# Attention keys in three bf16 parts: the stacks of parts laid out dimension by dimension, a row of ones filled by GpSimd, a batch of context requested by another queue

## The reference, cut to what matters

```python
def _L0_xattn_ref(q_vec, k_vec, v_vec, mask_input, Wq, bq, Wk, bk, Wv, bv, Wo, bo):
    ...
    q, k, v = proj(q_vec, Wq, bq), proj(k_vec, Wk, bk), proj(v_vec, Wv, bv)   # [b, head, row, 16]
    energy = jnp.einsum('bhqd,bhkd->bhqk', q, k) / jnp.sqrt(jnp.float32(D))
    energy = jnp.where(mask_input == 0, jnp.float32(-1000000000.0), energy)
    attn = jax.nn.softmax(energy, axis=-1)
    context = jnp.einsum('bhqk,bhkd->bhqd', attn, v)
    ...
x = x + _L0_xattn_ref(_layernorm(x), ctx_1024, ctx_1024, mask, ...)
x = x + _L0_attn_ref(_layernorm(x), ...)     # convolutions, gates
x = x + _L0_ffn_ref(_layernorm(x), ...)      # quantised feed forward
x = x + _L1_xattn_ref(...)                   # second cross attention
x = x + _L1_attn_ref(...)                    # attention with 16 heads of 64
x = x + _L1_ffn_ref(...)                     # 8 experts
```

## Time and profile before

| what | value |
|---|---|
| median of 3 runs | 941.09 us (939.6 to 942.02) |
| the profiled execution | 943.52 us |
| its span, first to last instruction | 941.7 us |
| TensorE busy | 893.4 us (95%) |
| VectorE, ScalarE, GpSimd busy | 605.6, 474.1, 107.8 us |
| mean granted TensorE clock | 0.986 |
| moved by DMA | 108.70 MB, mean 115 GB/s |

### The profile page before, as it was taken

One profiled execution on the slowest core, in us unless ns is written; L12 is line 12 of the kernel. 1 busy time (PEld: TensorE's weight loads), 2 busy tenths in 40 slices (PEclk: granted clock), 3 DMA queues, 4 the chain that ended last, 5 costly groups with the idle time before them and its releaser, 6 DMA issues.

```text
span 941.7 us, 15461 instructions
## 1 busy us (share of the span) xinstructions
PE 893.4 (95%) x6065; PEld 529.9 (56%) x6067; DVE 605.6 (64%) x1066; ACT 474.1 (50%) x953; POOL 107.8 (11%) x127
## 2 busy tenths in 40 slices
PE   7799799999999999999999999999999999999998
PEld 3356344444556665545445577754784884556745
DVE  5879478777886556888863387786724217459352
ACT  3242466777776566777779642314421310568311
POOL 2320011111000000000000200010100005335200
PEclk9899899999999999999999899999999999999999
DMA  9975733545322212222603620084645732000000
GB/s 294 302 223 164 219 107 96 154 122 168 107 68 80 68 34 60 76 67 70 210 8 129 259 71 1 1 266 137 223 179 187 260 100 79 1 1 1 1 0 23
DMA packets 68885, 108.70 MB, mean 115 GB/s; under 512 B 7110, under 2 KB 42950, under 8 KB 66886
## 3 DMA queue, kind: packets, MB, share of 16 engines
q1 hardware_dynamic: 65516, 100.61, 33.9%
q10 hardware_dynamic: 3296, 7.08, 2.2%
HBM read 93.77 MB, written 13.89 MB: 114 GB/s over the span
## 4 chain that ended last, share of the span: by engine, by line
PE 81%; DVE 7%; ACT 5%; DMA 3%; issue 2%; POOL 1%; SPq 0%; ACTq 0%; DVEq 0%
PE psum L1932 13%; PE psum L1914 11%; PE psum L1879 11%; PE psum L2312 6%; PE psum L1856 6%; PE psum L2340 6%; PE psum L2449 4%; PE psum L2073 4%; PE psum L1846 4%; PE psum L2086 3%; ACT arena L799 2%; PE psum L2503 2%; PE psum L2488 1%; PE psum L2527 1%; DVE arena L1202 1%
## 5 line engine op out<-in xcount | busy, mean ns | idle before, releaser
L1202 DVE TENSOR_REDUCE arena<-psum 128x1 f32<-128x1024 f32 x256 | 301.1, 1219 | 108.4 <-PE psum L1879 107.8
L799 ACT ACTIVATE arena<-psum 128x512 f32<-128x512 f32 x512 | 263.6, 603 | 68.2 <-PE psum L1914 67.0
L1879 PE MATMUL psum<-arena 96*128 96x512 bf16 x512 | 153.2, 381 | 9.5 <-DMA arena<-kparts 4.4
L1914 PE MATMUL psum<-arena 99*128 99x256 bf16 x1024 | 155.1, 274 | 3.5 <-ACT arena L790 1.2
L1932 PE MATMUL psum<-arena 128*32 128x256 f32 x2048 | 137.5, 386 | 0.1
L1914 PEld LDWEIGHTS psum<-arena 99*128 99x128 bf16 x1024 | 80.6, 97 | 98.2 <-ACT arena L799 36.7
L1932 PEld LDWEIGHTS psum<-arena 128*32 128x32 f32 x2048 | 53.5, 109 | 75.6 <-ACT arena L799 31.1
L1846 PE MATMUL psum<-arena 128*128 128x512 f32 x128 | 64.5, 632 | 11.9 <-DMA arena<-ctxT 10.5
L1879 PEld LDWEIGHTS psum<-arena 96*128 96x128 bf16 x512 | 48.9, 98 | 28.7 <-DVE arena L1202 11.4
L1856 PE MATMUL psum<-arena 128*128 128x256 f32 x256 | 64.1, 387 | 0.0
L673 POOL TENSOR_TENSOR arena<-arena 128x512 bf16<-128x512 f32 x34 | 41.4, 1217 | 196.4 <-DVE arena L1188 193.8
(11 more groups left out here) (259 smaller groups left out, 961.2 us busy)
## 6 DMA issues: line engine op xcount, KB each, us to landing
arena<-kparts SPq DMA_DIRECT2D x192, 128.0 KB, 3.1
kparts<-arena SPq DMA_DIRECT2D x32, 384.0 KB, 3.3
arena<-ctxT SPq DMA_DIRECT2D x20, 512.0 KB, 5.9
arena<-mask SPq DMA_DIRECT2D x8, 1024.0 KB, 5.4
arena<-ctx SPq DMA_DIRECT2D x2, 4096.0 KB, 17.0
arena<-mask ACTq DMA_DIRECT2D x4, 1024.0 KB, 13.9
arena<-ctxT SPq DMA_DIRECT2D x1, 4096.0 KB, 13.6
arena<-ctxT SPq DMA_DIRECT2D x4, 1024.0 KB, 9.1
```

The lines of the kernel that those rows point to most:

```text
L799: nc.scalar.activation(PR[step % 4][:, pair * CH:(pair + 1) * CH], exp_bank(step, pair), ACT.Exp)\
L1202: nc.vector.tensor_reduce(MX[g % 2][:, col:col + 1], unit_banks(n).rearrange("p b n -> p (b n)"), AX.X, ALU.max).then_inc(s_maxed, 1)
L1879: last = nc.tensor.matmul(out, q, KST[g % 2][0:ROWS, j, at], start=True, stop=not masked, skip_group_check=True)
L1914: last = nc.tensor.matmul(heads[:, u, :], KST[gg % 2][0:KROWS, j, kc * P:(kc + 1) * P], QST[0:KROWS, G * g + j, b * S:(b + 1) * S], start= ...
```

## The change

Keys and queries are projected with their features in the order dimension first, head second (`by_dim` permutes weights and biases on the host). `kparts` in HBM is now divided by quarter, with the rows of a quarter next to one another, so that the four heads of a group form one run of 4096 numbers for each dimension. The stack's rows are ordered by key part: 48 rows for the high part (dimension by dimension, three copies of each), 32 for the middle part, 16 for the low. One transfer brings all rows of a part, repeating each source row. So a quarter takes three transfers, and the queries likewise; the queries' three stores become one. The ones are no input any more: GpSimd fills them, the first time behind its other memsets, the second time behind the last low part of batch 0. The first six chunks of batch 1's context are requested by ScalarE, right behind its value copies. The matmuls keep their number and sizes.

```diff
+TWO_ONES = struct.unpack("<f", struct.pack("<I", 0x3F803F80))[0]
-K_PARTS = (0, 0, 0, 1, 1, 2)
-Q_PARTS = (0, 1, 2, 0, 1, 0)
+K_ROWS = ((0, 3), (3, 5), (5, 6))
...
-        KST = [b16(8192 * i, 16384).rearrange("p (j n) -> p j n", j=G) for i in range(2)]
+        KST = [b16(8192 * i, 16384).rearrange("p (c j n) -> p c j n", c=QUARTERS, j=G) for i in range(2)]
...
-        QST = b16(37392, 8192).rearrange("p (h n) -> p h n", h=H)
+        QST = b16(37392, 8192).rearrange("p (b h n) -> p b h n", b=B, h=H)
...
-        kparts = nc.dram_tensor("kparts", [B, 3, D, S2], BF16, kind="Internal").ap()
-        qparts = nc.dram_tensor("qparts", [3, D, T], BF16, kind="Internal").ap()
+        kparts = nc.dram_tensor("kparts", [B, QUARTERS, 3, D, 2 * CH], BF16, kind="Internal").ap()
+        qparts = nc.dram_tensor("qparts", [B, 3, D, S], BF16, kind="Internal").ap()
...
-            sp.dma_start(arena[ROWS:KROWS, 0:8192], t["ones"]).then_inc(q_stacked, 16)
...
             def store_k(b, c, f):
                 r = piece_number(b, c, f)
                 sp.wait_ge(k_low, r + 1)
-                sp.dma_start(kparts[b, :, f * P:(f + 1) * P, c * CH:(c + 1) * CH].rearrange("r p n -> p r n"),
+                sp.dma_start(kparts[b, c // 2, :, f * P:(f + 1) * P, c % 2 * CH:(c % 2 + 1) * CH].rearrange("r p n -> p r n"),
                              KPT[place(r)]).then_inc(k_stored[place(r)], 16)
...
             def load_stack(gg, quarter):
                 b, g = gg // GPB, gg % GPB
-                at = slice(quarter * 2 * CH, (quarter + 1) * 2 * CH)
-                for r in range(6):
-                    src = kparts[b, K_PARTS[r], g * G * DH:(g + 1) * G * DH, at]
-                    sp.dma_start(KST[gg % 2][r:ROWS:6, :, at],
-                                 src.rearrange("(j d) n -> d j n", d=DH)).then_inc(k_stacked[gg % 2][quarter], 16)
+                for part, (first, last) in enumerate(K_ROWS):
+                    src = kparts[b, quarter, part].rearrange("(d h) n -> d (h n)", d=DH)[:, g * G * 2 * CH:(g + 1) * G * 2 * CH]
+                    sp.dma_start(KST[gg % 2][first * DH:last * DH, quarter].rearrange("p j n -> p (j n)"),
+                                 src.unsqueeze(1).broadcast_to((DH, last - first, G * 2 * CH)))\
+                      .then_inc(k_stacked[gg % 2][quarter], 16)
...
             def store_queries(b):
                 r = query_piece(b)
                 sp.wait_ge(k_low, r + 1)
-                parts = KPT[place(r)].rearrange("p r (f n) -> p r f n", f=CT)
-                for part in range(3):
-                    sp.dma_start(qparts[part, :, b * S:(b + 1) * S].rearrange("(f p) n -> p f n", p=P), parts[:, part])\
-                      .then_inc(k_stored[place(r)], 16)
+                sp.dma_start(qparts[b].rearrange("r (f p) n -> p (r f) n", p=P),
+                             KPT[place(r)].rearrange("p r (f n) -> p (r f) n", f=CT)).then_inc(k_stored[place(r)], 16)
 
             def load_queries(b):
                 r = query_piece(b)
                 stored(r)
-                for r in range(6):
-                    src = qparts[Q_PARTS[r], :, b * S:(b + 1) * S]
-                    sp.dma_start(QST[r:ROWS:6, :, b * S:(b + 1) * S], src.rearrange("(h d) n -> d h n", d=DH))\
+                for first, last in K_ROWS:
+                    sp.dma_start(QST[first * DH:last * DH, b].rearrange("p h n -> p (h n)"),
+                                 qparts[b, 0:last - first].rearrange("r (d h) n -> d r (h n)", d=DH))\
                       .then_inc(q_stacked, 16)
...
             load_queries(1)
-            sp.dma_start(arena[ROWS:KROWS, 8192:16384], t["ones"]).then_inc(late_loaded, 16)
             sp.dma_start(BV, t["rows"][:, ROW_AT["bv"]:ROW_AT["bv"] + 256].broadcast_to((P, 256)))\
               .then_inc(late_loaded, 16)
             sp.dma_start(AW, t["A"].rearrange("(t p) s -> p t s", p=P)).then_inc(on["bm_loaded"], 16)
-            for c in range(SLOTS):
-                first_values_done(c + 2)
-                load_ctx(1, c, 0)
...
+            def ones_for_maxima(i):
+
+                nc.gpsimd.memset(arena[ROWS:KROWS, 8192 * i:8192 * (i + 1)], TWO_ONES).then_inc(built, 1)
+                pool.wait_ge(built, 9 + i)
+
+            pool.wait_ge(built, 8)
+            ones_for_maxima(0)
...
                 if idx == 2 * BRANCH - 1:
                     pool.wait_ge(q_split, 10)
                     low_part(query_piece(1), QREST)
+                if idx == 2 * NCH - 1:
+                    pool.wait_ge(k_low, r + 1)
+                    pool.wait_ge(mask_step, 8)
+                    ones_for_maxima(1)
...
             def load_queries():
 
                 act.wait_ge(k_stored[place(query_piece(0))], stores_by(query_piece(0)))
-                for row in range(6):
-                    act.dma_start(QST[row:ROWS:6, :, 0:S],
-                                  qparts[Q_PARTS[row], :, 0:S].rearrange("(h d) n -> d h n", d=DH)).then_inc(q_stacked, 16)
+                for first, last in K_ROWS:
+                    act.dma_start(QST[first * DH:last * DH, 0].rearrange("p h n -> p (h n)"),
+                                  qparts[0, 0:last - first].rearrange("r (d h) n -> d r (h n)", d=DH))\
+                       .then_inc(q_stacked, 16)
+
+            def load_next_ctx(c):
+
+                act.wait_ge(ring_drained, VALUE_AT[0, c + 2, 1] + 1)
+                n = load_number(1, c, 0)
+                act.dma_start(CTX[n % SLOTS], ctx_chunk(1, c)).then_inc(ctx_loaded[n % SLOTS], 16)
 
             for c in range(ROUNDS):
                 for i in range(2):
@@ -831,6 +844,8 @@
                         load_queries()
                     if c in VALUES_AT:
                         copy_values(0, VALUES_AT[c], i)
+                if c in VALUES_AT and VALUES_AT[c] >= 2:
+                    load_next_ctx(VALUES_AT[c] - 2)
...
-                    dve.wait_ge(late_loaded, 32)
+                    dve.wait_ge(late_loaded, 16)
...
-                    pe.wait_ge(q_stacked, 16 + 96 * (b + 1))
+                    pe.wait_ge(q_stacked, 48 * (b + 1))
                 if i % 8 == 0:
-                    pe.wait_ge(k_stacked[g % 2][quarter], 96 * (g // 2 + 1))
-                q = QST[0:ROWS, G * (g % GPB) + j, b * S + qt * P:b * S + (qt + 1) * P]
+                    pe.wait_ge(k_stacked[g % 2][quarter], 48 * (g // 2 + 1))
+                q = QST[0:ROWS, b, G * (g % GPB) + j, qt * P:(qt + 1) * P]
                 for half in range(2):
                     at = slice((2 * quarter + half) * CH, (2 * quarter + half + 1) * CH)
                     out = unit_banks(n)[:, half, :]
-                    last = nc.tensor.matmul(out, q, KST[g % 2][0:ROWS, j, at], start=True, stop=not masked,
+                    last = nc.tensor.matmul(out, q, KST[g % 2][0:ROWS, quarter, j, half * CH:(half + 1) * CH], start=True, stop=not masked,
...
                     pe.wait_ge(ring_drained, TOP_AT[gg, 1] + 1)
-                    if gg:
-                        pe.wait_ge(late_loaded, 32)
+                    pe.wait_ge(built, 10 if gg else 9)
...
-                        last = nc.tensor.matmul(heads[:, u, :], KST[gg % 2][0:KROWS, j, kc * P:(kc + 1) * P],
-                                                QST[0:KROWS, G * g + j, b * S:(b + 1) * S],
+                        last = nc.tensor.matmul(heads[:, u, :], KST[gg % 2][0:KROWS, kc // 8, j, kc % 8 * P:(kc % 8 + 1) * P],
+                                                QST[0:KROWS, b, G * g + j, :],
...
+    by_dim = np.arange(D).reshape(H, DH).T.reshape(-1)
+    cols = {"bq": a["L0_xattn_bq"][by_dim], "bk": a["L0_xattn_bk"][by_dim], "in_b": a["L0_attn_in_b"],
...
-        "wqT": c(a["L0_xattn_Wq"].T), "wkT": c(a["L0_xattn_Wk"].T), "wvT": c(a["L0_xattn_Wv"].T),
+        "wqT": c(a["L0_xattn_Wq"][by_dim].T), "wkT": c(a["L0_xattn_Wk"][by_dim].T), "wvT": c(a["L0_xattn_Wv"].T),
...
-        "ones": np.full((3, 8192), np.array([0x3F803F80], np.uint32).view(np.float32)[0], np.float32),
```

More of the change, by code:

```diff
@@ L1 @@
 import itertools
+import struct
 from contextlib import ExitStack
@@ L453, in stores_by @@
         def stores_by(r):
-            queries = sum(query_piece(b) <= r and place(query_piece(b)) == place(r) for b in range(B))
-            return 16 * (turn_at(r) + 2 * queries)
+            return 16 * turn_at(r)
         def stores_ahead(r):
@@ L705, in _ @@
             powers = [2 + 1]
-            pool.wait_ge(built, 9)
+            pool.wait_ge(built, 11)
             def power(first, last):
@@ L789, in copy_tops @@
                     act.wait_ge(ring_filled, slot + 1)
-                    nc.scalar.activation(QST[ROWS:KROWS, j:j + 2, b * S:(b + 1) * S],
+                    nc.scalar.activation(QST[ROWS:KROWS, b, j:j + 2, :],
                                          ring_heads(slot)[ROWS:KROWS], ACT.Copy).then_inc(ring_drained, 1)
@@ L2576, in _ @@
             pe.wait_ge(on["g_chosen"], 1)
-            pe.wait_ge(built, 11)
+            pe.wait_ge(built, 13)
```

(3 more changed lines are left out.)

## The result

The changed kernel takes 936.36 us (935.0 to 936.81, 6 runs), the kernel before 941.16 us (939.6 to 942.02, 6 runs). The ratio is 0.9948, 95% interval 0.9935 to 0.9961: faster by 4.8 us, where 11 were forecast. The profiled execution took 936.81 us with a span of 935.0, 6.7 us less than that of before. That execution of before lay 2.4 us above its median, so the traces differ by more than the medians; where the text follows a stretch, it follows the traces.

What follows compares the result with a forecast made beforehand. The prediction took TensorE, busy 893.4 of 941.7 us, as the bound, with gains only at its waits and low clock. Terms -5.0 - 6.6 + 0.6 = -11.0 gave a median of 930.0 us, range 926.5 to 937.

Steps and rivals of the forecast that it cites:

- B: TensorE's 4.31 us wait for context before the second batch's key projection at 109.19, plus half clock; claimed gain 6.6 us.
- The price of the last issue: ScalarE's last context issue, before the maxima copies that the product at 100.78 awaits; claimed +0.6 us, bounds 0.5 and 1.
- sign of danger: At the first turned product near 100 us: idle lengthening past 2 us and bringing the clock down would show the forecast wrong.
- GpSimd's fill: Filling 8192 words per partition twice, first from about 3.0 us; 8.4 us expected, cost 0, bounds 0 and +2.9.
- A's landing: Arrival of stacked keys and queries awaited before the first score product; claimed at 40.6 us, product then starting at 43.66.
- the term -5.0: Gain from three stack and query transfers instead of six, at the wait before the first score product; range 0 to -7.0.
- The ones: Dropping the two 96 KB transfers of ones was claimed to change nothing, as neither is in a TensorE wait.
- What is late next is VectorE: After the first score product, VectorE's splits and maxima set score unit 3; unit 4 starts at 49.9, not 54.89.
- only B goes: Rival: the first score product's wait hardly moves, because memory and engines pace it, not issues; 935 us, chance 0.17.
- The sentence from the Trainium skill on ports: Objection to the new rows: partitions 0 to 63 use 8 of 16 ports; 4.8 us for queries and quarter, landing at 41.1.

Runs made afterwards that it cites:

- e3: The kernel before with only the second batch's context moved to ScalarE's queue; 935.51 us, ratio 0.9941.
- e1: The changed kernel with the stacks' and queries' old rows and transfers, keeping GpSimd's ones and context on ScalarE's queue; 935.81 us, ratio 0.9943.
- e6: The changed kernel with six transfers of 16 rows without repetition, runs of 8 KB, written 6 partitions apart; 934.02 us, ratio 0.9923.
- e8: Old rows, GpSimd's ones and context on ScalarE's queue as in e1, plus batch 0's queries asked for earlier, at 28.7 us; 930.21 us, ratio 0.9875.
- e7: The same six transfers as e6, but each written to 16 neighbouring partitions; 937.8 us in a single run.
- e5: The changed kernel with batch 0's queries asked for earlier, behind the value copy at 28.7 us; 932.39 us, ratio 0.9904.
- e2: The kernel before with only the ones filled by GpSimd instead of transferred; 940.05 us, ratio 0.9981.
- e4: The kernel before with only the new rows, transfers and single query store; ones still transferred, context still on SP; 945.97 us, ratio 1.0063.

## Why the prediction was wrong, point by point

- **B, "Term: -6.6 us"**: right. From TensorE's end before it to the turned product behind it pass 2.81 us instead of 9.46, which is -6.65, and e3 has it alone.
- **The price of the last issue, "+0.6 us"**: right in mechanism; the idle grew by 0.42 us, with an issue of 0.38. What the term leaves out is the clock behind the longer idle. The prediction put its sign of danger at 2 us; in e1, e6 and e8 1.67 to 1.70 us were followed by the half clock and another 1.2 us.
- **GpSimd's fill, "I take 0"**: right. It took 6.92 us, not 8.4: a line through this fill and the 0.524 us of 512 words gives, as an estimate, 0.83 ns a word and a fixed 0.1 us, which the estimate had scaled too. It ended 5.9 us before the first low part.
- **The step that failed is A's landing**: "at 359 GB/s, which the window 44 to 46 shows, that is 4.4 us" and "with about 1 us to the end of the wait I put the landing at 40.6". It rested on a rate taken from a window in which no stack was loaded (44 to 46 us, packets of 1 KB on SP's queue). The new rows move at 188 GB/s where their window holds nothing else, e6 and e7 show that the partitions written decide this rate, and the queries landed at 42.9. So the term -5.0 was -0.2. Within it, "six issues take 4.1 of the 9 us" was read as a pace, which it was for the old rows only; the change took issues away and put transfers of neighbouring partitions in their place, and these took back what the longer runs gave.
- The second half of the same step: the queries were treated as landing with the stack. They are asked for at a place of their own, and once SP reached its stack 4 us earlier, its next stores came in between. e5 and e8 show that this place was worth 4 to 6 us: e5 -4.0 from the changed kernel, e8 -5.6 from e1 by the medians of different batches, -4.1 and -6.4 by the ratios.
- **The ones, "the two transfers go, at nothing: neither is in a TensorE wait"**: wrong. Not being waited for is no price. They slowed the mask's transfers and through them the stores, and SP's stack issue moved by 4.0 us (4.2 in e2, with the ones alone). In the changed kernel this gain was there and then lost at the queries, which had not moved.
- **"What is late next is VectorE"**, with unit 4 at 49.9: right where the landing was mended. In e8 it is VectorE that TensorE waits for, and unit 4 comes at 48.00. The 1.9 us between are those by which VectorE's last split before its maxima ends earlier (41.12 + 0.43 = 41.55 for 43.42), in a kernel that no longer loads the ones.
- **Rivals**: the one that came true in the main is "only B goes", 935 us at a chance of 0.17. Its reason, that memory and engines pace the landing and not the issues, comes near what the runs showed; it did not name the partitions or the place of the queries. The sentence from the Trainium skill on ports ("SBUF — State Buffer", section "Door 1: The DMA port swizzle (why `[64,N]` ≈ `[32,N]`)") pointed at the cause. It was worked out with stack and queries overlapping so well that every even port is always busy, 4.8 us for both together, and 41.1 looked harmless. One transfer after the other, that page's table puts 8 of the first 48 rows behind each of four ports, and 4 rows behind each port of the two smaller transfers: 2.4 + 1.2 + 1.2 = 4.8 us for a quarter and as much again for the queries, an estimate from that page's 27.2 GB/s. The trace agrees in direction and is somewhat faster: 188 GB/s in the window that holds only stack rows, which is 4.2 us for 768 KB. And in the trace the queries landed 5.1 us behind the quarter (42.9 for 37.8), not with it.

What stays open: that the ones were slow for the same reason as the dense rows (few neighbouring partitions) was not tried by itself. Shown is only that they were slow and what they held up. Open too is how much of the 2 us between e1 and e6 is issuing: five of the six query issues took 3.95 us in e1 and 3.40 in e6. And e7 has one run and no interval; it is read for its places, not for its time.

## What to carry to other kernels

Fewer, larger transfers are not faster if they write neighbouring partitions: look at which partitions one transfer covers, take its rate from a window with the same shape, and spread the rows (2 or 6 apart did it here). Long runs and spread rows are two separate gains, and a layout can win one while it loses the other. A transfer that nobody waits for can still hold up everything behind it; read the windows of full DMA share with low GB/s. When a wait ends on two transfers asked for by two queues, moving one forward gains nothing until the other moves, and it may put new work in front of it.

## What the runs showed that was not expected

- The share of DMA time says little of the bytes: 1.02 at 131 GB/s (e7), 1.02 at 423 GB/s (e2), 1.03 at 189 GB/s (changed, 80 to 100 us).
- The time that SP needs for an issue depends on the shape: six of the dense kind took 2.65 us (0.44 each), six with rows 6 apart 3.73 (0.62).
- 1.67 to 1.72 us of idle before the first turned product was followed by the half clock in three traces (e1, e6, e8) and not in six others; 1.25 us never was.
- SP asked for context 11 us earlier in e4 than before, and it was used 2.8 us later: an early issue behind slow transfers is a late one.
